# Moving a weight fetch behind four exponentials in a fused attention and routed-FFN kernel

## The reference, cut to what matters

```python
x = x + xattn(layernorm(x), ctx, ctx)      # 16 heads of width 16
x = x + ffn(layernorm(x))
# xattn: q, k, v projections; keys in 4 blocks of 64; softmax inside each block; a block of
#        queries sums the softmax outputs of the key blocks that a fixed pattern pairs with it
# ffn:   a shared MLP (256 -> 1024 -> 256, relu) for every token, plus one of two routed MLPs
#        of the same size, chosen per token by the larger of two gate scores
```

## Time and profile before

| | us |
|---|---|
| median of 3 runs | 1113.38 |
| the three runs | 1103.54, 1113.38, 1113.55 |
| the profiled execution | 1108.92 |
| its span, first to last instruction | 1107.1 |

### The profile page before, as it was taken

The page is one execution under the profiler, slowest core; times in us unless marked ns, Lnnn a source line. Parts: engine busy times, 40 slices in busy tenths (PEclk is TensorE's granted clock), DMA queues, the critical chain, the costliest instruction groups (busy, mean ns, idle before and its releaser), DMA issues.

```text
span 1107.1 us, 22039 instructions
## 1 busy us (share of the span) xinstructions
PE 894.2 (81%) x7751; PEld 739.1 (67%) x7751; DVE 534.3 (48%) x1090; ACT 447.6 (40%) x991; POOL 489.7 (44%) x798
## 2 busy tenths in 40 slices
PE   3477889988699696969969696987969698889897
PEld 2244667868577484948758494875849486677797
DVE  5657373746356381735537172653817264354300
ACT  3142524454435243443524343452434345244453
POOL 5443424464626254362625346262534526154453
PEclk8586888999999898998989898998989899899999
DMA  8675547566662817566381746548173664714800
GB/s 227 173 243 136 173 94 240 76 233 91 214 109 100 189 40 243 72 233 89 117 183 46 236 63 237 85 143 170 38 235 59 237 85 167 127 49 173 323 11 10
DMA packets 90481, 159.69 MB, mean 144 GB/s; under 512 B 8448, under 2 KB 80512, under 8 KB 85840
## 3 DMA queue, kind: packets, MB, share of 16 engines
q1 hardware_dynamic: 76432, 77.92, 34.2%
q10 hardware_dynamic: 4032, 58.72, 13.3%
q0 software_dynamic: 9984, 22.61, 7.1%
HBM read 119.84 MB, written 39.38 MB: 144 GB/s over the span
## 4 chain that ended last, share of the span: by engine, by line
PE 40%; DMA 22%; issue 12%; POOL 11%; DVE 10%; ACT 3%; SPq 1%; POOLq 0%; DVEq 0%; ACTq 0%
DMA scratch_q<-T 15%; PE acc L675 10%; PE hid L467 8%; POOL hl L1337 6%; PE num L540 5%; PE den L547 4%; PE work L467 3%; PE work L522 2%; PE work L587 2%; DVE nmax L1026 2%; POOL rstd L1329 2%; DMA rowin<-queue 2%; DMA queue<-rows,pos 2%; PE work L573 2%; POOL x1b L1344 1%
## 5 line engine op out<-in xcount | busy, mean ns | idle before, releaser
L1337 POOL TENSOR_TENSOR hl<-h,hh 128x256 fp32r<-128x256 f32 x272 | 202.1, 759 | 335.0 <-ACT hh L862 335.0
L841 ACT ACTIVATE PT<-work 128x512 f32<-128x512 f32 x256 | 131.2, 614 | 179.7 <-PE work L522 172.5
L1032 DVE COPY T<-num 128x512 f32<-128x512 f32 x64 | 44.2, 691 | 308.9 <-DMA scratch_q<-T 172.5
L1026 DVE TENSOR_REDUCE nmax<-work 128x8 f32<-128x512 f32 x256 | 162.4, 681 | 23.4 <-PE work L507 23.4
L540 PE MATMUL num<-PT,V 128*32 128x256 f32 x1024 | 78.9, 432 | 94.0 <-DVE T L1032 94.0
L522 PE MATMUL work<-QP,KP 128*128 128x256 f32 x512 | 107.1, 328 | 30.3 <-DMA QP<-scratch_m 20.1
L862 ACT ACTIVATE h<-hid,bias 128x256 f32<-128x256 f32 x160 | 78.1, 488 | 115.5 <-PE hid L467 115.5
L522 PEld LDWEIGHTS work<-QP,KP 128*128 128x128 f32 x512 | 76.5, 204 | 69.5 <-ACT PT L841 26.8
L507 PE MATMUL work<-KP,QP 96*128 96x512 f32 x256 | 97.9, 459 | 30.1 <-DMA QP<-scratch_q 17.7
L467 PE MATMUL hid<-XS,WS 128*128 128x256 f32 x768 | 110.5, 296 | 2.7 <-DVE idle L1194 2.7
L540 PEld LDWEIGHTS num<-PT,V 128*32 128x32 f32 x1024 | 28.9, 118 | 122.8 <-DVE T L1032 103.2
(11 more groups left out here) (238 smaller groups left out, 1638.8 us busy)
## 6 DMA issues: line engine op xcount, KB each, us to landing
WR<-wx ACTq DMA_DIRECT2D x28, 2048.0 KB, 11.6
KP<-scratch_k SPq DMA_DIRECT2D x96, 128.0 KB, 5.0
QP<-scratch_q SPq DMA_DIRECT2D x96, 128.0 KB, 8.1
scratch_k<-T SPq DMA_DIRECT2D x16, 512.0 KB, 3.3
scratch_q<-T SPq DMA_DIRECT2D x16, 512.0 KB, 15.5
wx<-WR POOLq DMA_DIRECT2D x16, 512.0 KB, 4.2
stages<-wraw POOLq DMA_DIRECT2D x24, 256.0 KB, 4.4
xin<-x SPq DMA_DIRECT2D x16, 256.0 KB, 9.4
```

The source lines that it names most:

```text
L841: nc.scalar.activation(PT[:, j % 8].rearrange("p t q -> p (t q)"), work[:, BANK[("st", j)], :], ACT.Exp).then_inc(sem["exp_done"], 1)
L1026: nc.vector.tensor_reduce(nmax[:, t, 8 * p:8 * p + 8], work[:, BANK[("s", j)], :].rearrange("q (b k) -> q b k", k=BLOCK), AX_X, ALU.max, n ...
L1032: nc.vector.tensor_copy(T[:, 2 * v:2 * v + 2, :], num[:, :, :]).then_inc(sem["num_copied"], 1)
L1337: nc.gpsimd.tensor_tensor(R(hl[:, k % 2, a]), h32[:, k % 2, a], hh[:, k % 2, a], ALU.subtract).then_inc(sem["hl_done"], 1)
```

## The change

The call of `load_weights(i)` on ACT moves from ahead of the first exponential of the pass to behind the fourth. Nothing else is altered; the waits inside `load_weights` stay as they are. It moves in the 14 passes that fetch, 2 to 15.

```diff
                 if more:
                     front_qk(i + 1)
-                if type(i) is not int or i >= 2:
-                    load_weights(i)
                 if type(i) is int and i == 0:
                     act.wait_ge(sem["proj_lo"], 4)
                 for j in range(4):
                     exps(i, j)
+                if type(i) is not int or i >= 2:
+                    load_weights(i)
                 for v in range(VISITS):
                     slot(i, 6 + v)
                     for j in range(4 * v + 4, min(4 * v + 8, HEADS)):
```

## The result

The changed kernel takes 1031.08 us in median (1025.89 to 1033.39), the kernel before 1110.26 in the same comparison: a ratio of 0.9288, 95% interval 0.9226 to 0.9349. I had forecast 1049, with a range of 1028 to 1080. The wait that I wanted gone is gone, and the gain was mis-sized: 79 us instead of 61. Ratios leave out executions over 1.5% above the fastest of their kernel.

What follows compares the result with a forecast made beforehand. The q write `scratch_q<-T`, landing only with the 4 MB fetch, was taken to bound 11 passes. 65.5 us gained in passes 4 to 14, less 2.2 and 3.4 lost, net 59.9 off 1108.92: 1049 us, range 1028 to 1080.

Steps and rivals of the forecast that it cites:

- The q wait at zero: DVE's first copy in passes 4 to 14 no longer waits for the q write; a caught pass cost 7.08 us more.
- The new place: Fetch issued behind the fourth exponential, about +3.55 us behind the q write instead of +0.34 (+0.11 in caught passes).
- The reads behind the fetch: Fetch lands at +17.0, 1.1 us later than in pass 3; `rowin`, the spreads and next scores move by that.
- 0 if the reads get in beside the fetch: Lower bound on the 1.1 us shift of `rowin`, spreads and next scores; the upper bound was +3.2.
- ACT's issue time: Two issues ahead of the fifth exponential put PE's visits 1.0 us later, covered by the 2.5 us to `rowin`.
- Passes 2, 3 and 15: Passes without a gain: 2.2 us lost in passes 2 and 3 together, 3.4 us lost in pass 15.
- The rule: Issue early, wait late: the fetch moves the wrong way, 45 us lost, 1154 us; chance counted with C's.
- Rival A: `rowin` and append get through ahead of the fetch, reads behind it don't move: 77.9 us less, 1031 us; chance 0.13.
- B: Fetch ends 3.2 us later, reads move with it, ACT's 1.0 us added: 61.2 us a pass, 1089 us; chance 0.13.
- C: The q write is still caught and lands with the fetch, 3.2 us later: 1168 us; chance 0.04.
- D: The wait was put down to the wrong releaser, another replaces it in full: within 1% of 1109; chance 0.04.

Runs made afterwards that it cites:

- lead alone: The kernel before, with the load of control into a register done twice (the extra load) ahead of the fetch: 1021.69 us, ratio 0.9214.
- less to fetch: The kernel before, with each of the fetch's two DMAs cut from 2 MB to 256 KB (the small fetch): 987.7 us, ratio 0.8877.
- the order reversed: The changed kernel, with SP issuing the q write only after the fifth exponential, behind the fetch (the late q write): 1174.9 us, ratio 1.0566.
- the one slow kernel with the residual moved: The kernel with the fetch behind the third exponential, with SP reading the residual tile right behind the q write: 1071.13 us, ratio 0.9581.

## Why the prediction was right or wrong

**The q wait at zero: right.** It is gone from the waits in all 11 passes, the write lands in 2.9 us, and the experiments settle the reason from four sides: lead alone (0.9214), less to fetch (0.8877), the order reversed (1.0566), and four later places that all free it. A lead of 0.34 us was enough in pass 3 before, and 0.55 to 0.70 us in passes 4 to 14 of the kernel with the extra load; the packets of passes 3 and 7 show how.

**The new place: right.** I expected the fetch at +3.55 behind the q write; it is at +3.2 to +3.4 in passes 4 to 14. Its second half was to land at +17.0: it lands 13.7 us after an issue at about +3.8 in pass 7, so at +17.5.

**The reads behind the fetch: the step that failed.** I had them move by 1.1 us with the fetch's end, to scores at 31.1 + 1.1 = +32.2. The fetch's end did move, by 1.6 us against pass 3, but the scores came at +30.5. That makes about 56.3 us of a pass instead of 58.1: 1.8 x 11 = 20 us, most of the 23 us by which the profiled execution is shorter than 1049. PE's waits behind the fetch, 0.4 us for `rowin` and 1.0 us for the spread in pass 7, are shorter than the 1.5 to 2.5 and 1.5 to 2.7 that I gave as signs. The error was to hold the stretch behind the fetch fixed. In pass 3, `rowin` reached PE 2.4 us and the scores started 15.2 us behind the fetch's end (248.8 to 251.24 and to 264.02). In pass 7 after, they are 0.9 and 13.0 us behind it (475.9 to 476.75 and to 488.93). Part of the reads is done beside the fetch. I had written that bound down ("0 if the reads get in beside the fetch") and taken the row of the case that I knew instead.

Other fetch ends say the same. SP issues the spread's first read once the last `scores_t` are done, ahead of the fetch's end. In pass 7 of three kernels (the extra load, the change, behind the eighth) that read is issued at +12.9, +12.7 and +12.1, the fetch ends at +15.6, +17.5 and +18.6, and the scores start at +31.2, +30.5 and +31.4. Over passes 4 to 13 the mean pass is 56.56, 56.28 and 57.53 us: 3 us more of fetch end cost 1.0 us of a pass, not 3.

Which read it is, is settled only in part. Issued late, `rowin` costs 1.1 us in a pass where the spread is the last to come, and 0.2 us on average. The append is the other transfer that no longer runs beside the fetch, but in the kernel with the extra load it still does (8.5 us), and passes are hardly longer there. What is shown is that the mean pass stays between 55.2 and 56.7 us for fetches issued about 0.6 to 3.4 us behind the q write, the one slow kernel with the residual moved left aside. With the small fetch it is 53.5 us, and the scores start at +27.6 without a wait, so what is above that comes with the full fetch. How PE and DMA share the 2.7 us, waiting for each other by turns, stays open.

**ACT's issue time: right in size in half of the passes, too small in the others.** In pass 7 the first copy starts at +6.58 instead of +5.58, the 1.0 us that I wrote. I called it hidden, and in the passes where PE then waits for `rowin` or the spread it is. But in passes 4, 6, 8, 10 and 12 the copy starts at +7.0 to +7.5, and there the pause of PE has a second price. Busy time of the engines in three stretches of pass 6 and one of pass 7 after (columns: stretch, its length, busy us and instructions of PE, PEld, DVE, ACT, POOL, then the granted clock, DMA share and GB/s):

```profile
398.00:404.00 6.00, 5.29 (x44) 4.93 (x43) 1.38 (x2) 2.69 (x5) 3.59 (x13) 1.00 0.52 171
404.00:410.00 6.00, 4.26 (x38) 2.48 (x40) 0.69 (x1) 4.11 (x9) 5.39 (x6) 0.79 0.84 264
410.00:416.00 6.00, 5.40 (x60) 3.09 (x50) 0.69 (x1) 3.04 (x7) 2.31 (x5) 0.93 1.02 386
...
460.40:466.40 6.00, 4.14 (x48) 2.67 (x46) 0.69 (x1) 4.19 (x10) 5.40 (x6) 1.00 0.80 267
```

In pass 6, TensorE's granted clock falls after this pause to a mean of 0.79, so part of the stretch is at the lower level (1.2 GHz); in pass 7 it stays at 1.00 (2.4 GHz). The last `scores_t` end 1.5 us later in pass 6: SP issues the spread 14.2 us behind the q write instead of 12.67. Such a pass is no longer than its neighbours (56.40 us against 56.37 in pass 7), since there PE comes last and in the others the spread does. With the fetch behind the third exponential PE has no such pause; only one or two of the passes 4 to 13 have a lower granted clock in its two traces. In pass 7 before, after PE had stood still for over 8 us, the mean granted clock from 498 to 520 us was 0.87. That is likely a part of the 7 us that a caught pass cost; how much of it was not measured.

**Passes 2, 3 and 15.** I had 2.2 us lost in the first two and 3.4 in the last. The stretch up to pass 4 became 0.8 us shorter. From the q write of pass 14 on, 4.5 us were gained, where pass 14 alone should give 7.1 by my price or 7.8 by the measured one, so pass 15 and what follows lost 2.6 to 3.3 us, near the forecast.

**The rule and the rivals.** The Trainium skill, "DMA: Bandwidth & Descriptors", section "Rules for kernel authors", says issue early and wait late. Within the places that give the lead, the runs agree with it: 1018 to 1021 us behind the first and the third exponential, 1031 behind the fourth, 1050 behind the eighth. It does not cover the step from 0.1 to 0.7 us behind the q write, which is worth 87 us the other way (1108.65 to 1021.69). Rival A had the right time (1031) and half of a reason: the reads behind the fetch hardly move, and the append and `rowin` do get ahead, but these two are not what pays. That its number meets the median so closely is luck in part, since it was counted from the profiled execution, which came to 1025.89. B's shift of the reads did not come; C's price was met in the kernel with the late q write; D is refuted by the result itself.

## What to carry to other kernels

When two transfers are issued within a few tenths of a microsecond on different queues, and the small one is waited for while the big one is not, look at their order first: here 0.6 us of lead for a 512 KB write of small rows over a 4 MB fetch took 8% off the kernel, slightly more than moving the fetch by four exponentials. Before pricing such an edit from the average pass, look for a pass in the trace that already has the other order; it gave the mechanism, and all of the size but the part in which I held the rest of the pass fixed. Put the issue of the transfer where its engine waits anyway, and do not assume that a third transfer moved beside the pair is free.

## What the runs showed of the hardware that I had not expected

- A write of 512 KB that takes 2.9 us with no fetch beside it took 15.1 to 15.7 us when a 4 MB read was issued 0.06 to 0.18 us behind it, 4.8 us at 0.34 us and 3.4 us at 0.7 us.
- While both transfers were under way, their packets went one for one (244 of 1 KB against 240 of 16 KB in 11 us). In pass 3, where the write had 0.34 us of lead, 466 of its 512 packets had started before the fetch's first.
- A 256 KB read issued behind the q write, 1.1 us ahead of the fetch, went with a second half of the fetch that landed in 16.8 to 18.9 us in six passes of ten and in 14.1 to 14.7 in the other four (1071 us instead of 1018). In the two other kernels with this edit it landed in at most 15.1 us in these passes.
- A pause of TensorE of 1.5 us was followed by a lower granted clock (0.79 over 6 us) in pass 6, and one of 1.6 us by no lower clock in pass 7, with the same instructions.
